# A fused recurrence and mixture-of-experts layer: the order of work at its start, in its first block and at its routed stage is changed

## The reference, cut to what matters

```python
# x, ctx: (16, 128, 512) float32
x = x + wkv(w, u, k=layernorm(x), v=ctx)      # a recurrence over 128 time steps
# per channel, in sequence (written with running maxima for stability):
#   y_t = (p + exp(u + k_t) v_t) / (q + exp(u + k_t))
#   p = exp(w) p + exp(k_t) v_t ;  q = exp(w) q + exp(k_t)
xf = layernorm(x).reshape(2048, 512)
gates = softmax(xf @ gate_w + gate_b)         # 16 experts, top 2 kept
routed = sum over the 2 experts e of gate_e * (gelu(xf @ ew1[e] + eb1[e]) @ ew2[e] + eb2[e])
shared = sum over 2 experts s of  gelu(xf @ sw1[s] + sb1[s]) @ sw2[s] + sb2[s]   # hidden 2048 each
return x + shared + routed
```

## Time and profile before

| What | Value |
|---|---|
| median of 3 runs | 889.35 us (886.95 to 891.01) |
| profiled execution: its own time | 888.09 us |
| profiled execution: span, first to last instruction | 886.5 us |
| busy: PE, DVE, ACT, POOL | 846.5, 636.9, 493.2, 183.7 us |
| mean granted TensorE clock | 0.984 of full speed |
| HBM traffic over the span | 149 GB/s |

### The profile page before, as it was taken

One profiled execution on the slowest core, in us unless ns is written; L12 is line 12 of the kernel. 1 busy time (PEld: TensorE's weight loads), 2 busy tenths in 40 slices (PEclk: granted clock), 3 DMA queues, 4 the chain that ended last, 5 costly groups with the idle time before them and its releaser, 6 DMA issues.

```text
span 886.5 us, 14887 instructions
## 1 busy us (share of the span) xinstructions
PE 846.5 (95%) x4054; PEld 702.0 (79%) x4054; DVE 636.9 (72%) x1339; ACT 493.2 (56%) x873; POOL 183.7 (21%) x223
## 2 busy tenths in 40 slices
PE   1589999999999999999999999999999899999998
PEld 1458788888888888888888888888888799987886
DVE  6976997856577788556687876555686688883855
ACT  6747676345366554445556463445455378885541
POOL 2100000112100000112000001110220577763850
PEclk9699999999999999999999999999999999999999
DMA  8353343368453333494433324555697367867976
GB/s 217 84 167 107 108 131 95 108 132 169 69 167 96 96 108 89 105 209 84 143 114 99 88 81 107 118 136 162 189 193 179 100 215 251 257 235 285 308 230 192
DMA packets 124592, 133.37 MB, mean 150 GB/s; under 512 B 10264, under 2 KB 86608, under 8 KB 124012
## 3 DMA queue, kind: packets, MB, share of 16 engines
q1 hardware_dynamic: 115020, 106.63, 44.9%
q0 software_dynamic: 8784, 25.11, 9.5%
q10 hardware_dynamic: 720, 0.81, 0.3%
HBM read 109.53 MB, written 22.98 MB: 149 GB/s over the span
## 4 chain that ended last, share of the span: by engine, by line
PE 92%; DVE 3%; issue 2%; ACT 1%; DMA 1%; POOL 1%; ACTq 0%; POOLq 0%; SPq 0%; DVEq 0%
PE up L591 13%; PE up L593 13%; PE up L592 13%; PE acc L653 12%; PE acc L658 12%; PE acc L655 12%; PE up L845 3%; PE up L847 2%; PE acc L591 2%; PE acc L593 1%; PE acc L592 1%; PE up L618 1%; PE misc L618 1%; PE misc L677 1%; PE up L754 1%
## 5 line engine op out<-in xcount | busy, mean ns | idle before, releaser
L591 PE MATMUL up<-xs,w1hi 128*128 128x512 f32 (+1 forms) x512 | 200.6, 392 | 1.9 <-issue 1.9
L593 PE MATMUL up<-xs,w1lo 128*128 128x512 f32 (+1 forms) x512 | 197.5, 386 | 0.0
L592 PE MATMUL up<-xs,w1hi 128*128 128x512 f32 (+1 forms) x512 | 197.1, 385 | 0.0
L653 PE MATMUL acc<-w2hi,hhi 128*128 128x512 f32 x494 | 192.8, 390 | 1.9 <-issue 1.9
L655 PE MATMUL acc<-w2lo,hhi 128*128 128x512 f32 x494 | 192.3, 389 | 0.0
L915 ACT ACTIVATE hhi<-up,b_col 128x512 fp32r<-128x512 f32 (+1 forms) x128 | 87.2, 682 | 152.7 <-PE up L593 122.0
L1176 DVE TENSOR_TENSOR hlo<-hf,hhi 128x512 fp32r<-128x512 f32 (+1 forms) x128 | 86.7, 677 | 87.0 <-ACT hf L918 51.2
L658 PE MATMUL acc<-w2hi,hlo 128*128 128x512 f32 x494 | 132.6, 389 | 0.0
L591 PEld LDWEIGHTS up<-xs,w1hi 128*128 128x128 f32 x512 | 96.2, 188 | 21.3 <-issue 2.7
L593 PEld LDWEIGHTS up<-xs,w1lo 128*128 128x128 f32 x512 | 96.2, 188 | 20.0
L592 PEld LDWEIGHTS up<-xs,w1hi 128*128 128x128 f32 x512 | 96.3, 188 | 18.6
(11 more groups left out here) (275 smaller groups left out, 1169.7 us busy)
## 6 DMA issues: line engine op xcount, KB each, us to landing
w_raw<-in_L_ffn_sw SPq DMA_DIRECT2D x266, 256.0 KB, 3.1
expert_rows<-ysb SPq DMA_DIRECT2D x47, 256.0 KB
xn_rows<-kn POOLq DMA_DIRECT2D x16, 256.0 KB, 8.5
e2raw<-in_L_ffn_ew SPq DMA_DIRECT2D x16, 256.0 KB, 5.1
ew_sb<-in_L_ffn_ew SPq DMA_DIRECT2D x16, 256.0 KB
X<-in_x SPq DMA_DIRECT2D x12, 256.0 KB, 9.4
vin<-in_ctx SPq DMA_DIRECT2D x12, 256.0 KB
out<-X SPq DMA_DIRECT2D x12, 256.0 KB, 4.4
```

The costliest lines, as they stand in the source:

```text
L591: nc.tensor.matmul(o, lhs[0], rhs[0], start=start, stop=False)
L592: nc.tensor.matmul(o, lhs[0], rhs[1], start=False, stop=False)
L593: return nc.tensor.matmul(o, lhs[1], rhs[0], start=False, stop=stop)
L653: nc.tensor.matmul(acc[t][:], hh, w2hi[:, slot], start=first and (q > 0 or t >= HT) or again, stop=False)
```

## The change

It has seven parts. (1) The two x loads of ScalarE's queue go to SyncE's. (2) In the prologue ScalarE does `wkv_reciprocal(1)` ahead of the early Gelus, with one load of the Gelu tables instead of two and no preload of the others; x_hi of the second half of the tokens goes ahead of split_w1(1), on VectorE x_lo likewise. (3) On TensorE result_T(2, 3) goes ahead of pre_down(1), and transpose_x(2, 3) ahead of pre_down(3). (4) SyncE waits for w1's places two chunks further on before it waits for w2's. (5) The half steps are 2, 5, 8, 11 and 14. (6) The recurrence's parts are dealt anew: one scan in part 4, the other in part 6. (7) TensorE waits for acc0 and acc1 directly ahead of the first down product of a slot; and in the last stage gathers and additions each come one step earlier.

```diff
-        wkv = Steps(sem("wkv"), "es ev h hv cq cp sp sq den num nt nr y ty")
+        wkv = Steps(sem("wkv"), "es h ev hv cq sq den cp sp num nt nr y ty")
...
-            if c < 2 * PRE:
-                return PRE + i // 2 if i % 2 == 0 else i // 2
+            if c < 3 * PRE:
+                return i // 3 if i % 3 == 2 else PRE + 2 * (i // 3) + i % 3
...
-            return isinstance(c, int) and c < 2 * PRE and c % 2 == 1
+            return isinstance(c, int) and c < 3 * PRE and c % 3 == 2
...
-            load_half(0, (0, 1))
+            load_half(0, range(GB))
...
-            for n in range(RING, PRE + RING):
+            def load_first(n):
                 if n < PRE:
                     load_pre_w1(n)
                 else:
                     sp.wait_ge(pre_up, n - RING + 1)
                     load_w1(n - PRE, n - PRE, chunk_of(n - PRE))
+
+            def load_second(n):
                 if n < PRE:
                     load_pre_w2(n)
                 else:
                     sp.wait_ge(pre_down, n - RING + 1)
                     load_w2(n - PRE, n - PRE, chunk_of(n - PRE))
+
+            load_first(RING)
+            load_first(RING + 1)
+            for n in range(RING, PRE + RING):
+                if n + 2 < PRE + RING:
+                    load_first(n + 2)
+                load_second(n)
...
             for p in range(PRE):
                 if p + 2 < PRE:
                     pre_up_product(p + 2)
-                if p == PRE - 1:
+                if p == PRE - 2:
                     for tb in range(HT, TB):
                         transpose_x(tb, xn[:, tb], acc[tb])
-                pre_down_product(p)
                 if p == 1:
                     for tb in range(HT, TB):
                         result_T(tb)
+                pre_down_product(p)
...
-            pe.wait_ge(acc_free, TB * (NQ - 1) + len(y_bank))
             for s in range(SLOT_TILES):
                 if s + 3 < SLOT_TILES:
                     routed_T(s + 3)
                 if s + 2 < SLOT_TILES:
                     routed_up(s + 2)
+                if s == 0:
+                    pe.wait_ge(acc_free, TB * (NQ - 1) + len(y_bank))
                 routed_down(s)
...
-            for g in (2, 3):
-                act.dma_start(X2[32 * g:32 * g + 32, 0, 0:HT], xq[0, g, :, 0:HT]).then_inc(x_half[0], 16)
...
-            pre_gelu(0)
-            pre_gelu(1)
-            nc.scalar.preload_act_table_set("natural_log_exp_and_others")
             wkv_reciprocal(1)
-            pre_gelu(2)
-            pre_gelu(3)
+            for p in range(PRE - 1):
+                pre_gelu(p)
             split_w1(0, 0)
-            pre_gelu(4)
-            split_w1(1, 1)
+            pre_gelu(PRE - 1)
             for tb in range(HT, TB):
                 x_hi(tb, 1, tb, acc[tb])
+            split_w1(1, 1)
             split_w1(2, 2)
...
             split_w1(0, 0)
             early_ln2_apply(1)
-            split_w1(1, 1)
             for tb in range(HT, TB):
                 x_lo(tb, 1, tb, acc[tb])
+            split_w1(1, 1)
             split_w1(2, 2)
...
-                    if n == 3 * k // 2 + 2:
+                    if n == 3 * k // 2 + 1:
                         take_rows(k)
...
-                pool.wait_ge(up_done, HOLD + 1 + 3 * k // 2)
+                pool.wait_ge(up_done, HOLD + 3 * k // 2)
```

More of the change, by code:

```diff
@@ L1375, in wkv_part @@
                     after(tabs, 0, "boost")
-                    after_last("sq")
+                    after_last("sp")
                     do(V.tensor_tensor(es[:, :, 1:], ek[:], grow[:, :, times], ALU.mult))
-                    after(wkv, r, "es")
+                    dve.wait_ge(x2_ok, TB + r)
+                    do(V.tensor_tensor(den[:], ek[:], boost[:, :, times], ALU.mult))
+                elif part == 3:
+                    after(wkv, r, "h")
                     after(wt, r, "tv")
                     do(V.tensor_tensor(ev[:, :, 1:], es[:, :, 1:], vp[:], ALU.mult))
[L1381 to L1384, removed]
                     after_last("y")
@@ L1388, in wkv_part @@
                 elif part == 4:
-                    after_last("num")
                     after(tabs, 0, "keep")
                     do(V.tensor_scalar(es[:, :, 0:1], qq[:, :, TH:], carry[:, bass.ds(s, 1)], None, ALU.mult))
-                    do(V.tensor_scalar(ev[:, :, 0:1], pp[:, :, TH:], carry[:, bass.ds(s, 1)], None, ALU.mult))
-                    after(wkv, r, "cp")
-                    do(V.tensor_tensor_scan(flat(pp[:]), flat(keep[:]), flat(ev[:]), 0.0, ALU.mult, ALU.add))
+                    after(wkv, r, "cq")
                     do(V.tensor_tensor_scan(flat(qq[:]), flat(keep[:]), flat(es[:]), 0.0, ALU.mult, ALU.add))
@@ L1399, in wkv_part @@
                                               op1=ALU.add))
+                    do(V.tensor_scalar(ev[:, :, 0:1], pp[:, :, TH:], carry[:, bass.ds(s, 1)], None, ALU.mult))
+                elif part == 6:
+                    after(wkv, r, "cp")
+                    do(V.tensor_tensor_scan(flat(pp[:]), flat(keep[:]), flat(ev[:]), 0.0, ALU.mult, ALU.add))
+                    after(wkv, r, "sp")
                     do(V.tensor_tensor(num[:], pp[:, :, 0:TH], num[:], ALU.add))
```

## The result

The changed kernel took 881.38 us (median of 8 runs, 879.35 to 884.16) against 890.58 for the kernel before in the same session (886.95 to 891.91): a ratio of 0.9903, 95% interval 0.9883 to 0.9923, or 6.9 to 10.4 us. 881.0 was forecast, 877.5 to 885.5 as the range. The profiled execution took 879.35 us with a span of 877.7, against 888.09 and 886.5.

A forecast was written before the change was run, and what follows sets the result against it. TensorE was taken as the bound, busy 846.5 of 886.5 us, so only its idle time could go. Terms 0.9 + 2.0 + 1.85 + 3.2 = 7.95 gave 880.1 or 881.4 us; forecast 881.0, range 877.5 to 885.5.

The forecast's parts named there:

- Part 1: Start of the prologue: with the x loads off ScalarE's queue the chain from wu comes 0.9 us earlier, bounds 0 and 0.92.
- its issue moves by all of it: Loads of wu: issued 0.92 us earlier, so the whole chain behind them was moved by 0.9.
- Parts 2 to 4: Rest of the prologue: up(0) starts at about 61.5 instead of 63.47, 2.0 us gained, bounds 0.8 and 2.4.
- Rival (c): Prologue: the reciprocal in front delays the Gelus, TensorE waits and the 2.0 us are lost; 883.0 us, chance 0.11.
- Parts 5 and 6: Block 0: TensorE's wait ahead of a down product goes, 1.85 us gained, bounds 1.85 and minus 1.
- Rival (b): Block 0: ScalarE's and VectorE's pace eats what the prologue gives, only 3.2 us stay; 885.8 us, chance 0.13.
- Part 7a: Start of the routed stage: the moved accumulator wait brings down(1) 3.2 us earlier, bounds 1.5 and 3.5.
- 1.5 are idle time and 1.7 the lower clock: Routed stage: how the 3.2 us divide, two waits of about 0.5 replacing 2.50 and no clock fall.
- Rival (a): Routed stage: the clock falls all the same, 1.7 us less gained; 882.7 us, chance 0.15.
- Part 7b: Last stage: earlier gathers and additions gain 0, as TensorE is full and the end hangs on the last Gelus.
- so 1.4 us of cover is left: Last stage: w2lo, behind the gathered rows' additions, ends at 822.5 and the down product starts at 823.96; cover was 3.5.
- Rival (d): Last stage: take_rows(0) waits for late gathers and holds up hlo, w2lo and TensorE; 890 us and more, chance 0.04.

The follow-up runs named there:

- e1: The kernel before with only the x loads moved from ScalarE's to SyncE's queue; no whole time given, wu's transpose at 5.23 us against 6.91.
- e2: The kernel before with the two x loads behind the wu loads in ScalarE's queue; no whole time given, wu's transpose at 5.61 us against 6.91.
- e11: The changed kernel with wkv_reciprocal(1) behind pre_gelu(1) again; no whole time given, first early up product to up(0) 24.66 us against 21.54.
- e12: The changed kernel with SyncE's order of loads as before; no whole time given, first early up product to up(0) 25.97 us against 21.54.
- e6: The changed kernel with half steps and recurrence parts both as before; no whole time given, up(0) to first routed transpose 633.23 us against 630.99.
- e3: The changed kernel with half steps at the odd places again; no whole time given, up(0) to first routed transpose 631.12 us against 630.99.
- e4: The changed kernel with both scans in part 4 of the recurrence again; no whole time given, first routed transpose to down(1) 13.43 us against 11.87.
- -5 alone: The changed kernel with only the new places of the half steps undone; profiled, not timed.
- -6 alone: The changed kernel with only the new dealing of the recurrence's parts undone, both scans in one part again; profiled, not timed.
- e5: The changed kernel with the wait for acc0 and acc1 ahead of the slot loop again; median 884.81 us, ratio to the kernel before 0.9937.

## Why the prediction was right, and where only by luck

**What bounds it, and the sum.** TensorE had idle places and the change takes them away. C (2.20 for 1.85) and E (0.14 for nothing) show no other bound from up(0) to the last routed product. 8.0 us were forecast; 8.7 came in the profiled executions, 9.2 between the timed medians.

**Part 1: 0.9, measured 1.7** (median of twelve against the one execution before; 2.03 in the execution shown). The step that failed is "its issue moves by all of it" as the whole of the term, with 0.92 as its upper bound: the landing is shorter too, most likely since 256 KB no longer stand ahead of wu in its queue (e1 and e2). The bound was taken from the issue alone and should have left part of the 3.55 of the earlier trace rows open.

**Parts 2 to 4: 2.0, measured 2.25 in the pair shown**, and 2.65 between the means of B: 24.35 of three with the old prologue (23.79, 24.47, 24.80) and 21.70 of nine with the new one (21.37 to 22.22; e11 and e12 left out). The upper bound of 2.4 holds where the early matmuls are quick (before and e6: 23.79 - 21.37). Where they are slow pre_gelu(1), and in the old order the reciprocal behind it, is late too. Otherwise the reckoning held: den has no idle ahead of it, pre_gelu(0) is in time. VectorE and ScalarE of the changed kernel:

```profile
44.11 1.23 DVE L1318 TENSOR_TENSOR num<-pp,num 128x1024 f32<-128x1024 f32 x1
45.25 1.22 DVE L1322 TENSOR_TENSOR den<-den,yy 128x1024 f32<-128x1024 f32 x1
```

```profile
42.69 1.28 ACT L1045 ACT_TABLE_LOAD   x1
43.98 0.84 ACT L1045 ACTIVATE hf<-up,b_col 128x256 f32<-128x256 f32 x2
```

The Gelu starts 1.29 behind the start of the table load. The Trainium skill's 2.66 us for a switch (ScalarE: Activation LUTs, section What ACT_TABLE_LOAD costs) would have put it at 45.35; the trace disagrees for this one, whose table load starts directly behind an activation. Rival (c) is out for the change as made, and e11 shows that its opposite was the danger. What the prediction missed is that the wait at up(0) also carried a risk: the clock fell behind it in e1 and e2, and both lost some 1.6 us by it, the kernel before did not.

**Parts 5 and 6: 1.85, measured 2.2**, less the 0.75 that part 6 brings at the end and that the prediction put at nothing. One of the two is surplus (e3, e4), and by the traces it should be part 6. The fall of VectorE's lead at steps 8 and 9 did no harm. Rival (b) is out: what the prologue gives arrives at the routed stage in full.

**Part 7a: 3.2, measured 3.18, and still wrong.** The place of down(1) was right to 0.04 us (11.83 reckoned, 11.87 measured). What failed is the split "1.5 are idle time and 1.7 the lower clock": I took the idle time removed as gained, but the two waits left are 0.75 and 1.22, not 0.5 each, as rlo takes 0.73 and not 0.28 (VectorE's row below), and every further wait has its restart. Against the same list at a kept clock (12.16) the edit gives 0.3, and 2.9 is a clock that falls in some executions of either kernel. A profile in which it fell was read as the rule. On the mean of the profiled executions the term is 1.0 to 1.2. The Trainium skill's reading (TensorE: Matmul & The Clock Gate, section What's actually happening), that the gate runs on its own time, fits here: equal waits of 2.5 us had both outcomes, and so had 0.75 + 1.22. Rival (a), put at 0.15, came in 3 of 9.

```profile
697.74 1.27 DVE L1779 TENSOR_TENSOR X<-X,acc 128x512 f32<-128x512 f32 x2
...
699.26 0.73 DVE L1768 TENSOR_TENSOR rlo<-rf,rhi 128x128 fp32r<-128x128 f32 x1
```

**Part 7b: 0, measured about -0.7** on the mean, not shown by the timed runs. The step "so 1.4 us of cover is left" was right in kind and too large, and the changed kernel shows none. I took the time at which 1.05 MB were through the earlier trace rows, 14.4 us behind the last routed product, for the landing of the first group. In the changed kernel 1.10 MB are through by then too, but the second group's gathers are already under way, and the first is whole only after 15.2 to 17.6. DMA queue of the changed kernel from 796 to 808.7 us:

```profile
q0 software_dynamic: 328, 1.10, 22.2%
```

Rival (d) is this mechanism. It needed 8 us to turn the result, and got at most 2.8.

With the means in place of the single values the sum is 1.7 + 2.65 + 2.2 + 1.2 - 0.7 - 0.75 = 6.3, and about 1.1 for the clock behind up(0) (1.6 in two of three), 7.4 in all. That stands inside the timed 6.9 to 10.4. The forecast of 7.95 was near because the underestimates of parts 1 to 5 and the overestimate of 7a, with the costs of 7b and part 6 that were put at nothing, about cancelled. That is luck.

**Open.** Why wu's landing varies by 0.9 between executions, and how often the clock falls behind each wait over many executions: some thirteen profiles give a share of a third or a half and no more. That -5 alone would be as quick, and -6 alone quicker by the 0.75 at the end, was not timed.

## What to carry to other kernels

Where one profile shows an idle time with a lower clock behind it, look at several executions before the clock's part goes into a sum: the idle time is the edit's, the fall is drawn anew each time. Price a wait from start to start, not by the idle column, and price a load in a queue by what stands ahead of it, in landing as well as in issue. An addition that waits for a DMA and stands in front of the splits that TensorE needs gets no cover from its mean arrival; put it one step later, where these traces show no cost. And look behind the last product too: here an edit in the midst of the kernel came with 0.75 us there.

## What was not expected of the hardware

The same 24 early up matmuls take 6.88 to 8.35 us over the fourteen profiled executions (6.91 before, 7.68 after), whatever the edit. In the changed kernel the granted clock is recorded as 1.00 all along, while four matmuls start per us at first and six later. Stretches of one us, columns: ends, length, busy (matmuls) of PE, clock, DMA share, GB/s:

```profile
39.00:40.00 1.00, 1.00 (x4) 1.00 0.00 0
...
44.00:45.00 1.00, 1.00 (x6) 1.00 0.04 11
```

The pitch is the lower level's in the first row (before, with 0.50 on record, it was 4 per us as well), so in a stretch this early the pitch is to be believed rather than the record. In the nine executions that have 0.50 on record there, the 24 matmuls take 5.4 us and half of the time that they spend at it: 6.88 with 2.9 us in e6, 8.35 with 5.9 in e5. So it is the clock's rise, and not the edit, that comes sooner or later. Of the 1.5 us between these two, B shows 0.85 (21.37 and 22.22): where TensorE is quick, as in e6, it waits 0.23 for VectorE's result.
